# The state-space spectrum product moved wholly to VectorE

## The reference, cut to what matters

```
Kf = jnp.fft.rfft(K, n=n, axis=-1)
xf = jnp.fft.rfft(x, n=n, axis=1)
y = jnp.fft.irfft(xf * Kf.T[None], n=n, axis=1)[:, :L]
return y + x * D_skip
```

```
x = x + _L0_xattn_ref(_layernorm(x), ctx_768, ctx_768, ...)   # 16 heads over 77 context rows
x = x + _L0_ffn_ref(_layernorm(x), ...)                       # 8 experts, the best 2 weighted
x = x + _L1_xattn_ref(_layernorm(x), ctx_768, ...)            # the text block
x = x + _L1_ffn_ref(_layernorm(x), L1_ffn_rhs)                # int8 matmul
```

## Time and profile before

| what | value |
|---|---|
| time, median of 3 runs | 632.68 us (632.57 to 633.1) |
| profiled execution: its time | 630.15 us |
| profiled execution: its span | 628.4 us |
| mean granted TensorE clock | 0.881 |
| PE, PEld busy | 476.6 us (76%), 309.7 us (49%) |
| DVE busy | 450.0 us (72%) |
| ACT, POOL busy | 230.6 us (37%), 137.5 us (22%) |

### The profile page before, as it was taken

The page is one execution under the profiler, slowest core; times in us unless marked ns, Lnnn a source line. Parts: engine busy times, 40 slices in busy tenths (PEclk is TensorE's granted clock), DMA queues, the critical chain, the costliest instruction groups (busy, mean ns, idle before and its releaser), DMA issues.

```text
span 628.4 us, 7915 instructions
## 1 busy us (share of the span) xinstructions
PE 476.6 (76%) x2499; PEld 309.7 (49%) x2499; DVE 450.0 (72%) x1770; ACT 230.6 (37%) x386; POOL 137.5 (22%) x182
## 2 busy tenths in 40 slices
PE   1665334498989999989999999999999955715360
PEld 1331013265745767644766655786766633413240
DVE  4259683763553458989688989979989689996516
ACT  2354441627333344453325355343463311401030
POOL 3502337157100030001421001222110050213110
PEclk9998565778998999999899999999999986667785
DMA  8609300000200003000003000000000000000000
GB/s 174 129 9 284 103 0 2 0 2 20 33 2 1 0 2 51 4 0 2 0 2 51 3 2 2 0 7 12 1 2 1 2 17 2 0 1 17 0 2 17
DMA packets 16156, 14.97 MB, mean 24 GB/s; under 512 B 1194, under 2 KB 14258, under 8 KB 16114
## 3 DMA queue, kind: packets, MB, share of 16 engines
q1 hardware_dynamic: 16114, 14.47, 10.6%
HBM read 9.15 MB, written 1.05 MB: 16 GB/s over the span
## 4 chain that ended last, share of the span: by engine, by line
PE 59%; DVE 23%; ACT 6%; issue 5%; POOL 3%; DMA 1%; SPq 0%; POOLq 0%; DVEq 0%; ACTq 0%
PE moe_y L783 17%; PE moe_h L771 16%; PE side L823 3%; PE side L726 3%; PE side L834 3%; PE side L842 2%; PE side L850 2%; DVE area L1221 2%; PE side L695 2%; PE side L811 1%; PE side L633 1%; DVE TOP L1211 1%; DVE M L1147 1%; PE side L797 1%; PE side L871 1%
## 5 line engine op out<-in xcount | busy, mean ns | idle before, releaser
L783 PEld LDWEIGHTS moe_y<-W,HT 128*128 128x128 f32 x1024 | 133.3, 196 | 47.3 <-issue 43.8
L771 PE MATMUL moe_h<-xnT_moe,W 128*128 128x512 f32 x256 | 136.4, 621 | 3.6 <-ACT HT L971 2.9
L783 PE MATMUL moe_y<-W,HT 128*128 128x128 f32 x1024 | 138.0, 281 | 0.0
L971 ACT ACTIVATE HT<-moe_h,W 128x512 f32<-128x512 f32 x128 | 87.3, 685 | 118.3 <-PE moe_h L771 118.2
L771 PEld LDWEIGHTS moe_h<-xnT_moe,W 128*128 128x128 f32 x256 | 42.5, 199 | 16.9 <-issue 10.2
L1490 POOL TENSOR_TENSOR area<-area 128x128 f32<-128x128 f32 x16 | 7.3, 455 | 175.5 <-ACT area L988 175.5
L1197 DVE SCALAR_TENSOR_TENSOR X<-moe_y,RW,X 128x128 f32<-128x128 f32 x128 | 35.9, 343 | 13.6 <-PE moe_y L783 13.4
L726 PE MATMUL side<-PT,VP 128*72 128x512 f32 x80 | 44.3, 640 | 0.4 <-ACT PT L953 0.4
L1221 DVE MATCH_REPLACE8 area<-TOP,area 128x77 f32<-128x77 f32 x192 | 40.6, 224 | 0.0
L1136 DVE TENSOR_REDUCE mx<-side 128x6 f32<-128x462 f32 (+1 forms) x48 | 24.5, 578 | 9.8 <-PE side L695 9.8
L953 ACT ACTIVATE PT<-side 128x512 f32<-128x512 f32 x40 | 23.6, 596 | 21.2 <-PE side L711 16.7
(11 more groups left out here) (312 smaller groups left out, 840.4 us busy)
## 6 DMA issues: line engine op xcount, KB each, us to landing
W<-in_w SPq DMA_DIRECT2D x8, 512.0 KB, 8.5
QA<-Q SPq DMA_DIRECT2D x24, 128.0 KB, 4.3
X<-in_x SPq DMA_DIRECT2D x4, 256.0 KB, 6.8
out_dram<-FO SPq DMA_DIRECT2D x4, 256.0 KB, 2.3
KM<-area SPq DMA_DIRECT2D x6, 160.0 KB, 5.6
V<-in_vpack SPq DMA_DIRECT2D x1, 579.0 KB, 8.0
area<-in_r2pack SPq DMA_DIRECT2D x1, 576.0 KB, 6.2
area<-in_gpack SPq DMA_DIRECT2D x1, 576.0 KB, 8.7
```

What stands on the lines that cost most here:

```text
L771: pe.matmul(moe_h[n % 2][:], W1[:, e, c * P:(c + 1) * P], xnT_moe[:, b % 2, :], start=True, stop=True).then_inc(moe_h_full, 1)
L783: mm = pe.matmul(moe_y[m % 2][:, t * P:(t + 1) * P], HT[:, m % 2, c, t * P:(t + 1) * P], W2[:, e, c, :], start=(c == 0), stop=(c == HC - 1))
L971: act.activation(HT[:, m % 2, c, :], moe_h[n % 2][:], ACT.Relu, bias=wc("b1")[:, e * HC + c:e * HC + c + 1]).then_inc(moe_h_ready, 1)
```

## The change

GpSimd's share of the spectrum step goes, and so does its semaphore yc_a. VectorE computes all of it, 14 instructions for each batch in place of 13. The four main products (XR by KR, XI by KI, XR by KI, XI by KD) each become one instruction of 512 columns, whose second operand is the distance-0 part of the kernel's spectrum broadcast over the two halves, shape (2, 2, 128) with a step of zero in the middle. Before, each was two instructions of 256 columns, one for each c. The waits inside the step are placed anew, and TensorE waits for y_a alone.

```
@@ pe, idft
-                    pe.wait_ge(y_a, 13 * (b + 1))
-                    pe.wait_ge(yc_a, 5 * (b + 1))
+                    pe.wait_ge(y_a, 14 * (b + 1))
@@ dve, spectrum
-                    def bc(k, c, dist):
-                        return k[:, c, dist:dist + 1, :].broadcast_to((P, NB, D))
-
-                    for c in range(2):
-                        dve.tensor_tensor(Ya[:, c], XR[:, c], bc(KR, c, 0), ALU.mult).then_inc(y_a, 1)
-                    for c in range(2):
-                        dve.tensor_tensor(YR[:, c], XI[:, c], bc(KI, c, 0), ALU.mult).then_inc(y_a, 1)
-
+                    def bc(k):
+                        return k[:, :, 0:1, :].broadcast_to((P, 2, NB, D))
+
+                    n = 14 * b
+                    dve.tensor_tensor(Ya[:], XR[:], bc(KR), ALU.mult).then_inc(y_a, 1)
+                    dve.tensor_tensor(YR[:], XI[:], bc(KI), ALU.mult).then_inc(y_a, 1)
+                    dve.tensor_tensor(Yb[:], XR[:], bc(KI), ALU.mult).then_inc(y_a, 1)
+                    dve.tensor_tensor(YI[:], XI[:], bc(KD), ALU.mult).then_inc(y_a, 1)
                     dve.tensor_tensor(Yc[:], XR[:, :, 0, :], KR[:, :, 1, :], ALU.mult).then_inc(y_a, 1)
                     dve.tensor_tensor(Yd[:], XI[:, :, 0, :], KI[:, :, 1, :], ALU.mult).then_inc(y_a, 1)
-                    dve.wait_ge(y_a, 13 * b + 6)
+                    dve.wait_ge(y_a, n + 4)
                     dve.tensor_tensor(YR[:], Ya[:], YR[:], ALU.subtract).then_inc(y_a, 1)
+                    dve.tensor_tensor(YI[:], Yb[:], YI[:], ALU.add).then_inc(y_a, 1)
+                    dve.wait_ge(y_a, n + 7)
                     dve.tensor_tensor(Yc[:], Yc[:], Yd[:], ALU.subtract).then_inc(y_a, 1)
-                    dve.wait_ge(y_a, 13 * b + 8)
-                    dve.tensor_tensor(YR[:, :, 1, :], YR[:, :, 1, :], Yc[:], ALU.add).then_inc(y_a, 1)
-
+                    dve.wait_ge(y_a, n + 8)
                     dve.tensor_tensor(Ya[:, :, 0, :], XR[:, :, 0, :], KI[:, :, 1, :], ALU.mult).then_inc(y_a, 1)
                     dve.tensor_tensor(Ya[:, :, 1, :], XI[:, :, 0, :], KD[:, :, 1, :], ALU.mult).then_inc(y_a, 1)
-                    dve.wait_ge(y_a, 13 * b + 11)
+                    dve.wait_ge(y_a, n + 9)
+                    dve.tensor_tensor(YR[:, :, 1, :], YR[:, :, 1, :], Yc[:], ALU.add).then_inc(y_a, 1)
+                    dve.wait_ge(y_a, n + 11)
                     dve.tensor_tensor(Ya[:, :, 0, :], Ya[:, :, 0, :], Ya[:, :, 1, :], ALU.add).then_inc(y_a, 1)
-                    dve.wait_ge(y_a, 13 * b + 12)
-                    dve.wait_ge(yc_a, 5 * (b + 1))
+                    dve.wait_ge(y_a, n + 13)
                     dve.tensor_tensor(YI[:, :, 1, :], YI[:, :, 1, :], Ya[:, :, 0, :], ALU.add).then_inc(y_a, 1)
@@ pool, spectrum: the whole step goes
-                    for c in range(2):
-                        pool.tensor_tensor(Yb[:, c], XR[:, c], bc(KI, c, 0), ALU.mult).then_inc(yc_a, 1)
-                    for c in range(2):
-                        pool.tensor_tensor(YI[:, c], XI[:, c], bc(KD, c, 0), ALU.mult).then_inc(yc_a, 1)
-                    pool.wait_ge(yc_a, 5 * b + 4)
-                    pool.tensor_tensor(YI[:], Yb[:], YI[:], ALU.add).then_inc(yc_a, 1)
```

More of the change, by code:

```diff
@@ L510, in recurrent_layers @@
         film_mul, xm_ready = sem("film_mul"), sem("xm_ready")
-        y_a, yc_a = sem("y_a"), sem("yc_a")
+        y_a = sem("y_a")
         s4_a, s4_ready = sem("s4_a"), sem("s4_ready")
```

## The result

The changed kernel takes 624.66 us (median of 6 runs, 622.79 to 625.53) against 632.43 us before (6 runs, 630.2 to 633.1). The ratio is 0.9881, 95% interval 0.9857 to 0.9906: 7.5 us faster, 5.9 to 9.0. The forecast was 5.5; the ratio applied to the 632.68 us that the prediction started from gives 625.2, near the fast end of its range. The profiled execution took 624.27 us, its span 622.5. Executions of one kernel differ in the course of the granted clock: 30 of the kernel before, in a later group of runs, had mean clocks of 0.862 to 0.881 and took 629.5 to 632.8 us, and the profiled one, at 0.881, is of the fastest kind.

The account below looks back on a forecast made before the run. No engine bounds throughout; the spectrum step on VectorE matters where its end is late. -1.27 - 1.82 - 1.82 - 0.58 = -5.49 us, profiled 630.15 to 624.66, median 632.68 to 627.2; range 624.8 to 630.0.

Parts of the forecast that it names:

- GpSimd was in the way: Spectrum step: GpSimd's simultaneous work costs VectorE about 3.2 us each time, 8.32 us against 5.12 in b = 1.
- rival E: Spectrum step: the change does less because GpSimd did useful work for free; given no chance of its own.
- The length of the step, 6.50: VectorE's 14 new instructions last 6.50 us, against 8.32 where the old step meets GpSimd: 1.82 us less.
- Rival D: Spectrum products: broadcasting over a middle dimension halves VectorE's rate, step 8.94 us, kernel +1.9 us, 634.5; chance 0.03.
- rival B: Spectrum step: each instruction costs its whole duration start to start, step 7.50 us, -2.46 us in all, 630.2; chance 0.10.
- b = 0, -1.27: Router behind batch 0's spectrum: TensorE's 1.27 us idle time at L753 goes, carried whole to the end.
- rival A: Batch 2's inverse transform: no clock effect, so -4.91 us in all, 627.8; chance 0.22.
- rival C: Tail: the clock moves stretches by 1.44 us either way; -2.6 (630.1, chance 0.10) or -8.4 (624.3, chance 0.08).
- b = 1, 0: Batch 1: VectorE ends about 1 us ahead, but TensorE sets the pace, so no gain.
- b = 2, -2.40: Batch 2: -1.82 us from the shorter step TensorE waits for, -0.58 from VectorE's wait for the inverse transform.
- The wait of 0.58: VectorE's L1285 wait in batch 2 goes: the inverse transform starts before the clock falls, more at 2.4 GHz; -0.58 us.
- b = 3, -1.82: Batch 3: TensorE waits for the step's end with nothing else left, so the whole 1.82 us is gained.

Follow-up runs that it names:

- the products in halves: The changed kernel with its four main products split again into eight of 256 columns, VectorE alone; 625.47 us, ratio 0.9889 against the kernel before.
- the kernel with unused products: The changed kernel plus GpSimd computing its former five instructions into a buffer nobody reads; 635.15 us, ratio 1.005 against the kernel before.
- the kernel with b = 3 alone: The kernel before with the new spectrum step in batch 3 only, the old step in the other three; 630.32 us, ratio 0.9982.

## Why the prediction was right, and where it was short

- **GpSimd was in the way.** Right, and shown from both sides: without it 6.42 us (6.69 with the products in halves), with it and nobody waiting 9.6 us in b = 0 and 3. The remark under rival E that GpSimd's part was free nowhere that VectorE was busy is too strong: in b = 2 of the kernel with unused products it cost VectorE 0.40 us.
- **The length of the step, 6.50.** Right: 6.42. Broadcasting over the middle dimension costs nothing (0.68 to 0.69 us for 512 columns, as without it). Rival D (half rate) fell, and so did rival B: starts are 0.60 apart for instructions of 0.69, so an independent instruction does not cost its whole duration here. The bound of 0.874 for a product was not reached.
- **b = 0, -1.27.** This is the term that was mis-sized: -2.9 (-3.9 to -1.8). The wait at L753 went as predicted. "I carry the 1.27 whole" was the weak step: it took the later work as unchanged by the shift, and the forward transform of b = 2 changed by 1.64, of which 1.43 passed on. The prediction named such an effect twice, in rival A (all that TensorE did before is 1.27 earlier) and in rival C, but gave it no term and could not tell its sign. The measured 7.5 lies nearer to rival C with a gain (8.4) than to the forecast (5.5); which way the clock went was luck.
- **b = 1, 0.** Right within what can be told: -0.4 (-1.0 to 0.3).
- **b = 2, -2.40.** -1.8 (-2.5 to -1.1) alone, an interval that holds the forecast; in the pair of profiles 2.57 us. The wait of 0.58 did go, but not for the reason given. The clock fell before the transform began (0.80 over 510 to 512 us, 0.50 until 518, 0.99 after), so the start of the transform ran at the lower level; it took 5.75 because the clock rose about 4.1 us after its start.
- **b = 3, -1.82.** -1.1 (-2.0 to -0.3), which holds the forecast too. TensorE's wait is 1.83 shorter in the changed kernel, as forecast; the transform behind it took 0.58 longer there, and 0.94 longer in the kernel with b = 3 alone (6.07 for 5.13). Since it took 5.13 to 6.66 in the kernels where b = 3 was left as it was, the change in b = 3 can't be held to be the cause. This is rival C with its sign against us, in a smaller size.
- **624.66.** The prediction has this figure for the profiled execution, which took 624.27. That the measured median is 624.66 as well is chance: its forecast was 627.2.

## What to carry to other kernels

Before giving half of an elementwise step to GpSimd, look at how long VectorE's own instructions take beside it: where both read SBUF one of them is held, or they take turns, and 5 us of help cost VectorE over 3 us. A small shift early in this kernel went with another clock level in a matmul stretch 180 us later, so a sum over stages is safe in its mechanism and not to within a microsecond or two. And where one engine waits for a whole step, let it start on the part that is ready: VectorE starting on XR and TensorE on YR gave 4.4 us on top of the 7.5, part of it through the clock.

## What the runs showed that was not expected

- Two GpSimd products of 256 columns took 1.5 us where VectorE was the one held, 1.84 where they took turns with VectorE's of the same size, and 7.65 where VectorE was already running without a gap.
- The forward transform of b = 2 took 3.67 us or 5.3 us (5.31 to 5.36) in all 14 profiles and nothing between, sorted by the time from the forward transform of b = 0.
- TensorE kept busy through its gap kept the 2.4 GHz level, and the kernel gained nothing that can be told (0.9821 against 0.9811).
